# A longer pause of the maxima around a router, and one turn per step: a change to the order of work in an attention kernel with experts

## What is computed

```python
xn = _layernorm(x)
s  = _L0_attn_ref(xn, ...)          # attention, 16 heads of 8, causal; layernorm; projection
g  = _silu(_L0_ffn_ref(xn, ...))    # attention with rope, 4 shared k/v heads; gate; then experts
x  = x + s * g

# the second branch, behind its attention:
h2     = rmsnorm(x, ln2_w)
logits = h2 @ Wr + br
top1   = argmax(logits)                       # one of 8 experts for each token
u      = h2 @ W1[top1] + b1[top1]             # 128 -> 512
act    = u1 * sigmoid(u2)                     # 256
y      = act @ W2[top1] + b2[top1]            # 256 -> 128
return x + y
```

## Time and profile before

| | |
|---|---|
| runs | 805.2, 807.17, 812.69 us (median 807.17) |
| profiled execution | 805.09 us, of which its span 803.4 us |
| TensorE busy | 729.2 us, 91% of the span |
| ScalarE, VectorE, GpSimd busy | 579.5, 558.7, 185.0 us |
| mean granted clock of TensorE | 0.963 of full speed |
| chain that ended last, by engine | PE 72%, DVE 16%, ACT 5%, issue 5%, DMA 1% |

### The profile page before, as it was taken

One profiled execution on the slowest core, in us unless ns is written; L12 is line 12 of the kernel. 1 busy time (PEld: TensorE's weight loads), 2 busy tenths in 40 slices (PEclk: granted clock), 3 DMA queues, 4 the chain that ended last, 5 costly groups with the idle time before them and its releaser, 6 DMA issues.

```text
span 803.4 us, 28715 instructions
## 1 busy us (share of the span) xinstructions
PE 729.2 (91%) x12293; PEld 335.4 (42%) x12293; DVE 558.7 (70%) x1488; ACT 579.5 (72%) x682; POOL 185.0 (23%) x356
## 2 busy tenths in 40 slices
PE   1388999999999999999999999989999999999994
PEld 1243343434443444444434444443443434466652
DVE  6977345888787777767688777667878667445436
ACT  1177887778777887888778768766777568787882
POOL 4363113101121102110211031010310334225241
PEclk9589999999999999999999999999999779999997
DMA  4222342042030002000300021000000041445423
GB/s 123 61 64 64 123 139 83 2 79 74 6 118 3 3 2 78 3 3 2 113 10 2 3 80 42 2 3 2 3 3 2 16 159 41 112 115 165 151 61 92
DMA packets 33876, 44.29 MB, mean 55 GB/s; under 512 B 6502, under 2 KB 26342, under 8 KB 33750
## 3 DMA queue, kind: packets, MB, share of 16 engines
q1 hardware_dynamic: 32358, 39.62, 16.8%
q0 software_dynamic: 1248, 2.57, 0.9%
q10 hardware_dynamic: 144, 0.27, 0.1%
HBM read 31.88 MB, written 10.24 MB: 52 GB/s over the span
## 4 chain that ended last, share of the span: by engine, by line
PE 72%; DVE 16%; ACT 5%; issue 5%; DMA 1%; POOL 0%; POOLq 0%; DVEq 0%; ACTq 0%
PE PS L1000 25%; PE PS L978 22%; PE PS L948 14%; PE PS L907 7%; ACT PR L881 5%; DVE MP L1304 4%; DVE PS L1301 2%; PE PS L1010 1%; DVE KA L1225 1%; DVE OT L1324 1%; DMA XN<-in_x 1%; DVE QA L1205 0%; DVE KA L1187 0%; DVE HS L1215 0%; PE PS L1097 0%
## 5 line engine op out<-in xcount | busy, mean ns | idle before, releaser
L881 ACT ACTIVATE PR<-PS 128x1024 f32<-128x1024 f32 (+1 forms) x576 | 531.1, 976 | 126.6 <-PE PS L978 123.9
L978 PE MATMUL PS<-QA,KA 74*32 74x512 bf16 (+3 forms) x5120 | 336.3, 353 | 8.9 <-ACT PR L881 8.3
L1304 DVE TENSOR_REDUCE MP<-PS 128x1 f32<-128x512 f32 x384 | 255.4, 690 | 81.3 <-PE PS L948 80.2
L1000 PE MATMUL PS<-PR,VA 128*18 128x512 f32 (+3 forms) x2560 | 289.5, 535 | 1.4 <-POOL PR L703 0.9
L948 PE MATMUL PS<-KA,QA 72*32 72x512 bf16 (+3 forms) x2560 | 231.2, 354 | 13.0 <-DVE MP L1304 6.8
L703 POOL TENSOR_SCALAR_AFFINE_SELECT PR<-PR 128x256 f32<-128x256 f32 x256 | 103.1, 420 | 447.1 <-ACT PR L881 441.2
L978 PEld LDWEIGHTS PS<-QA,KA 74*32 74x32 bf16 x5120 | 129.3, 97 | 167.5 <-ACT PR L881 74.8
L1301 DVE CUSTOM_DVE_ANT_0 PS<-PS,CON 128x128 f32<-128x128 f32 (+3 forms) x256 | 124.2, 503 | 45.2 <-PE PS L948 42.2
L948 PEld LDWEIGHTS PS<-KA,QA 72*32 72x32 bf16 x2560 | 70.4, 95 | 134.6 <-DVE MP L1304 54.3
L1000 PEld LDWEIGHTS PS<-PR,VA 128*18 128x18 f32 x2560 | 72.3, 99 | 52.5 <-issue 15.4
L1301 DVE DVE_READ_ACCUMULATOR2_ANT MP<- 128x1 f32 x256 | 36.3, 142 | 0.0
(11 more groups left out here) (170 smaller groups left out, 377.8 us busy)
## 6 DMA issues: line engine op xcount, KB each, us to landing
QA<-q_parts SPq DMA_DIRECT2D x96, 96.0 KB
QA<-in_W SPq DMA_DIRECT2D x16, 450.0 KB, 3.3
KA<-k_parts SPq DMA_DIRECT2D x48, 96.0 KB
KA<-in_W SPq DMA_DIRECT2D x7, 450.0 KB
q_parts<-QA SPq DMA_DIRECT2D x4, 384.0 KB, 2.6
q_parts<-KA SPq DMA_DIRECT2D x4, 384.0 KB, 3.8
expert_tokens<-ZERO SPq DMA_DIRECT2D x1, 1483.5 KB, 10.8
QA<-expert_tokens SPq DMA_DIRECT2D x1, 1483.5 KB, 8.6
```

Source lines behind the costliest of these rows:

```text
L881: act.activation(PR[:, (2 * n + p) % RING, :, 0:w], PS[:, 2 * p:2 * p + 2, 0:w], ACT.Exp)\
L978: last = pe.matmul(PS[r:r + STRIP, hh, start:start + CH - q0], KA[0:ROWS, b, kb // BPC, 0 if ffn else hh, key:key + STRIP], QA[0:ROWS, b, ...
L1000: last = pe.matmul(PS[STRIP * hh:STRIP * hh + 2 * VW, 6, q0:CH], VA[:, slot % 2, kb, hh, VW * (1 - place):VW * (3 - place)], PR[:, (2 * n ...
L1304: dve.reduce_max(top, bank, AX).then_inc(s_mr, 1)
```

## The change

Four things are done.

1. `SCATTER` is one step later (236), `EXPERTS` stays at step 238, and `HOLD` is steps 231, 235 and 236. So the two steps that `places` runs beside carry no maxima.
2. A step in `HOLD` no longer counts in the shares. No step has a burst: 232, 233, 234 and 237 have 3 units of full width each.
3. A shift turn no longer shares a step with a piece of `FFN_AT`, another shift turn or a turn of outputs; it goes to the next step that is free. T10 moves from step 182 to 183, T11 from 204 to 205, T12 from 209 to 210, T13 from 219 to 220, and T14 from 236 to 235, since its units now end one step earlier (233).
4. The tokens are loaded in six transfers, five of four tiles and one of three, each with a semaphore of its own. Piece E of four tiles waits for one of them; `output_rows` waits for all six.

```diff
+PIECES = (NT + 3) // 4
 ...
-SCATTER = ROUTED + 5
-EXPERTS = SCATTER + 3
+SCATTER = ROUTED + 6
+EXPERTS = SCATTER + 2
 ...
-HOLD = (ROUTED + 1, ROUTED + 5)
+HOLD = (ROUTED + 1, ROUTED + 5, ROUTED + 6)
 ...
     for a, (first, end) in enumerate(MAX_SPAN):
-        total = sum(width(SEQ[n][1]) + 400 for n in range(first, end))
+        total = sum(width(SEQ[n][1]) + 400 for n in range(first, end) if n not in HOLD)
         work = HG * sum(item_width(i) + 64 for i in range(len(ITEMS)))
         u = done = own = 0
         for n in range(first, end):
-            own += width(SEQ[n][1]) + 400
             if n in HOLD:
                 continue
+            own += width(SEQ[n][1]) + 400
             while u < UNITS and (n == end - 1 or done * total < own * work):
 ...
     for c in range(NC):
-        SHIFT_AT.setdefault(maxima_end(a, c) + 2, []).append(("T", NC * a + c))
+
+        n = maxima_end(a, c) + 2
+        while n in FFN_AT or n in SHIFT_AT or ended(n - LAG - 1) is not None:
+            n += 1
+        SHIFT_AT[n] = [("T", NC * a + c)]
 ...
-        s_xs = sem("expert_tokens_loaded")
+        s_xs = [sem(f"expert_tokens_loaded_{k}") for k in range(PIECES)]
 ...
-                    sp.dma_start(XS, XGD.rearrange("(j p) n -> p j n", p=P)).then_inc(s_xs, 16)
+                    rows = XGD.rearrange("(j p) n -> p j n", p=P)
+                    for i in range(PIECES):
+                        j = slice(4 * i, min(4 * i + 4, NT))
+                        sp.dma_start(XS[:, j, :], rows[:, j, :]).then_inc(s_xs[i], 16)
 ...
-                    pe.wait_ge(s_xs, 16)
+                    pe.wait_ge(s_xs[k], 16)
 ...
-                dve.wait_ge(s_xs, 16)
+                for i in range(PIECES):
+                    dve.wait_ge(s_xs[i], 16)
```

## The result

| | kernel before | the change |
|---|---|---|
| median of 11 runs each | 807.73 us (805.2 to 814.73) | 804.36 us (801.69 to 806.38) |
| ratio | | 0.9947, 95% interval 0.9922 to 0.9973 |
| profiled execution | 805.09 us, span 803.4 | 804.85 us, span 803.0 |

The account below looks back on a forecast made before the run. TensorE's work at its granted clock, plus its gaps, was taken to bound the kernel. 805.09 - 10.0 - 0.8 - 3.3 + 0.4 = 791.4, plus 0.6 for the median, said as 792 us; range 787 to 802.

Parts of the forecast that it names:

- Turns moved: Shift turns T10 to T13 in later steps: waits for them go or shrink, -3.3 us, bounds -4.5 and -1.9.
- Maxima spread: Up to step 230, 91 units instead of 87: VectorE's added reductions cost +0.4 us, bounds 0 and 2.7.
- The wait itself: Step 236: TensorE's 1.70 us wait for VectorE goes, net -0.8 us after T14's new wait, bounds -1.7 and 0.
- T14 next: End of step 235: T14 becomes the next late piece, waiting about 0.9 us for bank 7.
- Scatters and tokens: Scatters a step later, tokens in six loads: last load lands before its use, cost 0, 4.3 us of slack.
- the rival: Tokens late: VectorE in step 258 waits for six loads if they run in series; 808 us, chance 0.05.
- Clock: Slow stretch 631.8 to 652.3 us: clock stays up, saving half of 20.02 busy us, -10.0 us.
- Nothing else takes over at once: In the slow stretch: VectorE and ScalarE, busy 15.86 and 15.79 of 20.50 us behind it, leave room for the gain.
- The base: Starting point of the sum: the kernel before's profiled execution, 805.09 us.
- the clock falls all the same: Around T14's wait, in two steps without maxima, the clock still falls: 801 us, chance 0.15.
- near 0.9 the clock holds, at 1.7 it falls: At T14's wait: a wait near 0.9 us leaves the clock up, one of 1.7 us brings it down.

Follow-up runs that it names:

- e1: The changed kernel run again with no edit: 804.72 us.
- e5: The kernel before run again with no edit: 808.82 us (one run).
- e4: The change with GpSimd's scatters of tokens and of outputs left out: 791.53 us.
- e6: The kernel before with GpSimd's scatters of tokens and of outputs left out: 796.68 us.
- e2: The change without its fourth part, the tokens loaded in one transfer again: 804.76 us.
- e3: The kernel before with only the change's fourth part, the six token loads: 806.92 us, ratio 0.9982.
- g2: The kernel before with the scatters of tokens starting three steps later, at step 238: 808.74 us.
- e7: The change with expert outputs stored by plain 64 KB transfers from SP instead of GpSimd's scatters: 796.54 us.
- g3: e8 plus one joint TensorE signal per expert step (second product first in plain steps) and token scatters started at their own step's scores: 794.23 us.
- e8: The change with the scatters of tokens two steps later, from step 238 on: 800.05 us.
- g1: The change with expert outputs stored by plain transfers issued by GpSimd instead of its indexed scatters: 796.33 us.

## Why the prediction was wrong

The start of a step in the change against the kernel before, in three pairs of traces, each less the difference at step 182, ahead of all that was changed (us, negative is earlier):

| step | first traces | e1 and e5, both with late signals | e4 and e6, without scatters |
|---|---|---|---|
| 220 | -2.5 | -2.4 | -2.5 |
| 228 | -0.6 | -0.6 | -0.6 |
| 237 | -6.0 | -5.5 | -5.6 |
| 238 | -5.1 | -3.0 | -5.4 |
| 242 | -7.6 | -3.3 | -5.7 |
| 258 | -6.8 | -2.7 | -5.1 |
| 287 | -0.1 | -2.7 | -5.1 |

- **Turns moved (-3.3): right.** -2.5 at step 220, inside the bounds; the two waits that stayed, O2's and W2's, gave 0.6 and 0.3 us back where 0.7 each was taken.
- **Maxima spread (+0.4): mis-sized.** From step 220 to 228 1.9 us are given back in all three pairs, inside the bounds 0 and 2.7. In the first traces TensorE is busy there for 20.50 us in the change against 19.44, and waits for VectorE 1.2 us against 0.3: the added units cost on both engines, where the term counted VectorE's reductions alone. Step 236 loses its five units in return; what that gives was not measured by itself.
- **The wait itself (-0.8), T14 next: right.** T14 waits 0.72.
- **Scatters and tokens (0): right for the tokens** (e2, e3). In the change the six loads had landed by 684.18, 8.7 us behind the first issue, where the rival allowed 12.9 us and worked out 19.8, or 15.5, for six in a row. For the scatters the term asked only when the last one lands. That the first ones, ready behind the chain of places, come in a burst was to be seen (in the first trace of the kernel before they start at 631.76, 633.94 and 635.23); that they touch TensorE was not.
- **Clock (-10.0): this step failed.** Its mechanism was right: the units brought the clock down (g2, e6), and with them gone it stays up (e4). "Nothing else takes over at once" was wrong: the scatters did, with a stand of TensorE's signals of 2 to 3 us, and the clock fell once more. And its size came from one long fall. By the term's own rule, half of the slow time, the windows above make the fall worth 1.7 us in e6 and 1.7 + 3.4 = 5.1 us in e5, not 10.0. In the pair without scatters, where the change has all that it was meant to have, steps 236 to 258 bring 5.1 - 0.8 = 4.3 us (step 236 is 0.8 ahead there), with the wait and the five units that left step 236 included, where 10.8 were forecast.
- **The base (805.09): this failed too, unseen.** The sum took the first trace for the kernel. It was an execution with a long slow clock and no late signal among the experts (59.00 us for steps 266 to 284, against 65.03 in e5). The change is 6.8 us ahead of that trace at step 258 and loses it all to late signals; e5, the kernel before run again, loses some 6 us there too, so beside e5 the change keeps its 2.7. By the medians it is 3.4. The first trace's total looked usual, 805.09, since its longer slow stretch and its missing late signals nearly cancel: that is chance, and it hid both.

Of the 13.7 us that were forecast against the first trace 0.1 is left at step 287. By the first column 0.8 is missing with the turns, 1.5 with the maxima, 4.6 with the wait and the clock (6.2 came of 10.8, from step 228 to 258), and 6.7 among the experts.

The rival "the clock falls all the same" (801, chance 0.15) named the right event with the wrong cause: it was to come from T14's wait. What the prediction held against it does not carry beyond its trace: the waits of the earlier trace rows left the clock at 1.00 there, in the change and in e5, but in e4, e7, g2 and g3 the clock fell at that place (0.83 from 50 to 60 us), behind a wait of 1.04 or 1.05 us for GpSimd that is as long in the change. So "near 0.9 the clock holds, at 1.7 it falls" could not be had from one trace. The rule of the Trainium skill that stood beside it ("TensorE: Matmul & The Clock Gate", "A second HAM failure mode: psum-queue depth-cycling"), short idle times without a long gap, finds both in these traces: in e8 the hole, two steps without maxima, left the clock at 1.00; in e5 the clock, back at 1.00 in between, fell a second time, and before that fall its timeline has only these short waits, among narrow units:

```profile
641.38 0.24 PE L948 MATMUL PS<-KA,QA 72*32 72x128 bf16 x4 [0.36 <-DVE MP L1304]
642.91 0.24 PE L948 MATMUL PS<-KA,QA 72*32 72x128 bf16 x4 [0.86 <-DVE MP L1301]
```

```profile
638.60:642.00 3.40, 2.96 (x56) 1.33 (x48) 2.59 (x6) 2.96 (x3) 1.62 (x2) 1.00 0.06 19
...
645.50:648.90 3.40, 3.40 (x32) 1.47 (x28) 1.89 (x3) 2.05 (x2) 0.10 (x1) 0.50 0.89 278
```

That second place was hidden inside the 20.5 slow us of the first trace, where the clock was low from the first wait on; no experiment was made on it.

## What to carry to other kernels

Before a sum is made against one trace, ask whether the stages that the change does not touch ran as they usually do; a second profile of the unchanged kernel would have shown 6 us here. The same holds for rows that are to speak against a rival. Where consumers idle for "issue" or "remote" while TensorE's matmuls are recorded as done, look at what GpSimd does beside them, and move its indexed scatters apart from each other and away from signals that others wait for. When a wait is taken from in front of a queue, list what else becomes ready at the same moment: here the clock stayed up only when both bursts, of units and of scatters, were gone.

## What was not expected of the hardware

GpSimd's indexed scatters make TensorE's signals late: with them left out (e4, e6) no signal between 630 and 785 us comes more than 0.12 us behind the modelled end of its matmul, and in e1 40 of 268 come more than 0.2 us behind it, by up to 0.9 us beside a single scatter and up to 2.8 us beside three in a row. How late one comes hangs on when it is due. In e1 33 of the 49 signals due 0.5 to 1.3 us behind a scatter's start are late, and those beside one scatter come 1.3 to 1.6 us behind its start (due at 0.59, 0.83 and 1.02: come at 1.42, 1.49 and 1.58), later than the end of the 0.96 us that GpSimd is busy with it. Nearly all that are due earlier come at once. Why the other 16 of the 49 are in time is not known. Plain transfers of the same size hold nothing (e7, g1).

The Trainium skill ("SBUF — State Buffer", "Who interferes with whom") says, of the ports to that memory, that PE and ACT never wait on anyone; what is late here is TensorE's signals, by the 0.2 to 2.8 us above, and no run shows whether a port has to do with it. What the scatter and the signal share was not shown.

Nor is it known why the first trace of the kernel before has none of this: of its 56 signals due 0.5 to 1.3 us behind a scatter's start none comes more than 0.2 us late, while the same kernel in e5 has late signals, as have the first trace of the change and all traces with scatters from the four chips of these experiments.
